# TensorE sums the three tiles of exponentials of a cross-attention itself, and the output product stands two score pairs later

## The chip, the core and the metric

The kernel runs on one core of one Trainium2 chip. The time is what the device takes for one launch, in microseconds (us). Five engines work side by side on this core: TensorE (PE) multiplies matrices and writes to PSUM, VectorE (DVE) and ScalarE (ACT) read PSUM and SBUF, GpSimd (POOL) reads SBUF, and SyncE (SP) issues most of the transfers. They wait for each other by semaphores only.

## What is computed

The reference is two layers on 16 items (B) of 112 rows (SQ) and 256 columns (D), with a context of 375 rows (SK) for each item:

```python
x = x + L0_xattn(layernorm(x), ctx)      # attention without softmax
x = x + L0_ffn(layernorm(x))             # 8 experts that choose their tokens
x = x + L1_xattn(layernorm(x), ctx)      # the part that the change touches
x = x + L1_ffn(layernorm(x))
# L1_xattn, H = 16 heads of width 16
scores = einsum('bhqd,bhkd->bhqk', Q, K) / sqrt(16)
weights = softmax(scores, axis=-1)
attn = einsum('bhqk,bhkd->bhqd', weights, V)
return attn @ Wo.T + bo
```

The change concerns the softmax's sums over the context rows and the product with `Wo`.

## The kernel before

The four parts of the two layers follow each other as stages. Within the stage of the second attention, everything goes step by step over the 16 items; n counts the steps. All engines' programs are written out by hand, in the order in which they run, and an engine runs its own list strictly in that order, waiting where a semaphore has not reached its count. Names such as `exp1_done` are semaphores.

Each item needs two kinds of scores. First come the maxima over the context: TensorE makes scores with the 112 queries on the partitions, two heads at a time (`score(n, j)`, a *score pair*, j = 0 to 7, L1559), and VectorE reduces each pair to its maxima (`two_max`, L1448). Pairs use PSUM banks 0 and 1 for even j, 2 and 3 for odd j; a pair waits until the maxima of the pair two before it are taken (`max_done`). When all eight are there, TensorE turns the maxima (`shift_turn`, the *turn*, L1566), ScalarE and VectorE form a shift (L1341, L1456), and ScalarE spreads it into extra rows of the queries `qpk` (`spread_shift`, L1344). This happens for item n+1 while item n is in the second kind of work.

Second come the weights: TensorE makes the scores again, transposed, with the context rows on the partitions (`transposed_scores`, L1582). One *unit* is four heads of one tile of 125 context rows; 12 units u = 0 to 11 make an item: for each half m of the heads, three tiles t with two groups g. ScalarE takes the exponential of each unit into `probs` (L1363). Units use three PSUM banks in turn, so unit u waits for exponential u-3. TensorE multiplies `probs` by the values, 24 matmuls for each half m (`weigh(n, m)`, L1595), into bank 7. Each such matmul uses 32 columns of the array, and four of them, g = 0 to 3, stand side by side. An f32 matmul leaves two records in the profile, so `weigh` has 48 a half.

The sums over the context are made in two parts. GpSimd adds the three tiles of a half elementwise: `half_sum` from tiles 0 and 1 (L1287), `tile_sum` from that and tile 2 (L1293), both in `add_tiles`. TensorE then folds `tile_sum` over the partitions with a table `halves` as weights (`add_up(n, m)`, a *fold*, L1608), 8 matmuls a half, into `sums` in bank 7. `add_up(n, 0)` stands at the end of step n, `add_up(n, 1)` after unit 1 of step n+1.

The rest of item n happens in step n+1. VectorE takes the reciprocal of `sums` (`invert_sums`, L1471) ahead of maximum 2, multiplies (`normalise`, `au`, L1478) ahead of maximum 3; ScalarE adds a bias after exponential 5 (`add_bias`, `aT1`, L1353); TensorE makes the product with `Wo` (`out_product`, the *out product*, L1618) into columns 384 to 511 of banks 0 and 1; and VectorE adds it to `x_all` (`add_x`, L1464).

The order is set by the numbers at the top of the program. `SCORES_AFTER` says after which unit which score pair of item n+1 stands: pair 2 after unit 2, 3 after 4, 4 after 6, 5 after 8, 6 after 10. `OUT_AT = 4` puts the out product just ahead of pair 4, and `ADD_AT = 5` puts `add_x` ahead of maximum 5. Pair 1 opens a step, pair 7 and pair 0 of item n+2 stand after `weigh(n, 0)`, then the turn, `weigh(n, 1)` and `add_up(n, 0)`.

SyncE loads the keys and queries of item n+3 once the units of step n are done; three slots of `kpk` and `qpk` are used in turn (`AHEAD`).

Of the kernel before, what the change touches and what calls it, by code (L numbers as in the profile page):

```python
# [17 lines left out]
ALU = mybir.AluOpType  # L18
# [37 lines left out]
SCORES_AFTER, OUT_AT = {2: 2, 4: 3, 6: 4, 8: 5, 10: 6}, 4  # L56
INVERT_AT, NORM_AT, ADD_AT = 2, 3, 5
# [42 lines left out]
def two_layer_kernel(nc, d, out):  # L100
# [1048 lines left out]
    tile_sum = sb(ctx, "tile_sum", [KT, KC, HC * SQ])  # L1149
    half_sum = sb(ctx, "half_sum", [KT, KC, HC * SQ])  # L1150
# [37 lines left out]
    tile_sum_done = sem(ctx, "tile_sum_done", 2 * KC)  # L1188
    pv_ps = sem(ctx, "pv_ps", KC)
    sums_ps = sem(ctx, "sums_ps")  # L1190
# [69 lines left out]
    def _(pool):  # L1260
# [21 lines left out]
        def add_tiles(n):  # L1282

            each = UNITS // KC
            for m in range(KC):
                pool.wait_ge(exp1_done.sem, exp1_done.at(n, each * m + 4))
                pool.tensor_tensor(half_sum[:, m], probs[:, m, 0], probs[:, m, 1], ALU.add)\  # L1287
                    .then_inc(tile_sum_done.sem, 1)
                pool.wait_ge(tile_sum_done.sem, tile_sum_done.at(n, 2 * m + 1))
                pool.wait_ge(exp1_done.sem, exp1_done.at(n, each * (m + 1)))  # L1290
                if n:
                    pool.wait_ge(sums_ps.sem, sums_ps.at(n - 1))
                pool.tensor_tensor(tile_sum[:, m], half_sum[:, m], probs[:, m, 2], ALU.add)\  # L1293
                    .then_inc(tile_sum_done.sem, 1)

        pool.wait_ge(qp3_done.sem, qp3_done.at(PAIRS - 1))
        for n in range(B):
            add_tiles(n)
            ahead(n)

    @block.scalar
    def _(act):
# [53 lines left out]
        def step(n):  # L1356
            for u in range(UNITS):
                m, t, g = unit(u)
                act.wait_ge(st_ps.sem, st_ps.at(n, u + 1))
                if t == 0 and g == 0 and n:  # L1360
                    act.wait_ge(pv_ps.sem, pv_ps.at(n - 1, m + 1))
                    act.wait_ge(tile_sum_done.sem, tile_sum_done.at(n - 1, 2 * (m + 1)))
# [12 lines left out]
        act.wait_ge(set_up.sem, set_up.at(0))  # L1375
        zero_padded(0)
# [132 lines left out]
    def _(pe):  # L1509
# [91 lines left out]
        def add_up(n, m):  # L1601

            pe.wait_ge(tile_sum_done.sem, tile_sum_done.at(n, 2 * (m + 1)))
            if m == 0 and n:
                pe.wait_ge(rsum_done.sem, rsum_done.at(n - 1))
            for h in range(2):
                for g in range(4):
                    ins = pe.matmul(sums[32 * g:32 * g + 32, m], halves[:, h],  # L1608
                                    tile_sum[:, m, (2 * g + h) * SQ:(2 * g + h + 1) * SQ],
                                    start=(h == 0), stop=(h == 1), tile_position=(0, 32 * g))  # L1610
            if m == KC - 1:
                ins.then_inc(sums_ps.sem, 1)
# [9 lines left out]
        def step(n):  # L1622
# [3 lines left out]
            for u in range(UNITS):  # L1626
                transposed_scores(n, u)
                if u == 1 and n:
                    add_up(n - 1, 1)
# [476 lines left out]
```

## Time and profile before

| | |
|---|---|
| median of 3 runs | 869.42 us (863.68 to 872.46) |
| profiled execution, whole | 868.87 us |
| profiled execution, span of the profile | 867.1 us |
| mean granted TensorE clock | 0.96 |
| busy in the span: TensorE | 760.4 us (88%) |
| VectorE | 477.2 us (55%) |
| GpSimd | 306.4 us (35%) |
| ScalarE | 299.4 us (35%) |

The span is the stretch from the first to the last recorded instruction; the whole execution is 1.8 us longer. All starts in this document count from the start of the span. The stage of the second attention lies between about 443 and 681 us. "PE" are matmuls, "PEld" the weight loads that overlap them. A row of the timeline merges neighbours of one kind: its "us" is from the first one's start to the last one's end, and the end of a matmul is modelled, so the time from one row's start to the next one's is what an entry takes in TensorE's queue. The releaser named behind an idle time is the one that ended last by the profile; it can be wrong where several are waited for.

### The profile page before, as it was taken

To read this page: it belongs to the slowest core of one execution; us is meant where nothing else is said; L and a number is where in the kernel's file an instruction comes from. 1 tells how busy PE (TensorE), PEld (TensorE's weight loads), DVE (VectorE), ACT (ScalarE), POOL (GpSimd) and SP (SyncE) were. 2 spreads that over 40 slices of the span, in tenths; PEclk is the share of its full clock that TensorE was granted. 3 is DMA by queue.
4 is the path that set the end of the run, shared out by engine and by line. 5 is a ranking of instruction groups with operands and counts; after the bars stand their busy time and mean duration, and the time that the engine had idled before them with its cause. 6 is when DMAs were issued, how large, how long until landed. Compare 5 with 4: busy or idle time off the path is not lost. (4 is left out here: it accounts for less than half of the span.)

```text
span 867.1 us, 16326 instructions
## 1 busy us (share of the span) xinstructions
PE 760.4 (88%) x6177; PEld 619.4 (71%) x6177; DVE 477.2 (55%) x1262; ACT 299.4 (35%) x628; POOL 306.4 (35%) x229
## 2 busy tenths in 40 slices
PE   3999999949998999996687878878788599999997
PEld 1566666624587988985666767667676489999997
DVE  1577667668860422304756677776665444555552
ACT  0111111117822311222347666665667022222221
POOL 1233332227830332316325766666666100000000
PEclk9999999969999989999898999999999699999999
DMA  9893000124785643533624776575670000000000
GB/s 284 305 170 44 22 22 22 43 68 145 205 163 107 211 140 123 164 73 86 126 48 79 127 125 124 94 134 90 121 201 2 1 1 12 12 12 11 11 11 22
DMA packets 64468, 81.46 MB, mean 94 GB/s; under 512 B 31890, under 2 KB 54802, under 8 KB 62834
## 3 DMA queue, kind: packets, MB, share of 16 engines
q1 hardware_dynamic: 61042, 70.84, 35.5%
q0 software_dynamic: 2816, 3.67, 2.4%
q10 hardware_dynamic: 544, 6.03, 2.0%
q8 instruction: 46, 0.75, 0.4%
q14 instruction: 20, 0.16, 0.1%
HBM read 60.45 MB, written 19.31 MB: 92 GB/s over the span
## 5 line engine op out<-in xcount | busy, mean ns | idle before, releaser
L1448 DVE TENSOR_REDUCE mx<-psum 112x2 f32<-112x750 f32 x128 | 116.1, 927 | 64.8 <-PE psum L1559 64.8
L1363 ACT ACTIVATE probs<-psum 125x448 f32<-125x448 f32 x192 | 91.6, 545 | 24.7 <-PE psum L1582 24.3
L507 PE MATMUL psum<-wkv,ctx_all 128*125 128x512 f32 x192 | 88.0, 609 | 13.2 <-DMA wkv<-in_wkv 13.2
L1287 POOL TENSOR_TENSOR half_sum<-probs 125x896 f32<-125x896 f32 x32 | 66.5, 2079 | 83.7 <-ACT probs L1363 83.7
L507 PEld LDWEIGHTS psum<-wkv,ctx_all 128*125 128x125 f32 x192 | 36.1, 193 | 54.2 <-issue 37.9
L1582 PEld LDWEIGHTS psum<-qpk,kpk 128*125 128x125 bf16 x768 | 64.2, 142 | 14.1 <-issue 4.4
L1769 ACT ACTIVATE relu<-psum,cols 128x224 f32<-128x224 f32 x64 | 28.7, 448 | 122.5 <-PE psum L1966 122.5
L1582 PE MATMUL psum<-qpk,kpk 128*125 128x112 bf16 x768 | 67.6, 227 | 3.2 <-ACT probs L1363 1.5
L1293 POOL TENSOR_TENSOR tile_sum<-half_sum,probs 125x896 f32<-125x896 f32 x32 | 66.9, 2090 | 2.5
L1559 PE MATMUL psum<-kpk,qpk 96*112 96x375 bf16 x256 | 63.2, 338 | 5.0 <-issue 2.4
L1098 PE MATMUL psum<-we,hT 128*112 128x256 f32 x256 | 61.2, 401 | 0.0
L1962 PE MATMUL psum<-hnT,wi 128*128 128x224 f32 x256 | 59.0, 353 | 1.1 <-DVE bias_row L1918 1.1
L1982 PE MATMUL psum<-wo,hs 128*112 128x256 f32 x256 | 58.2, 380 | 0.0
L1747 POOL TENSOR_TENSOR rs<-ve,mhalf 112x2 f32<-112x2 f32 x8 | 5.6, 698 | 145.1 <-DVE ve L1798 145.1
L1098 PEld LDWEIGHTS psum<-we,hT 128*112 128x112 f32 x256 | 47.7, 189 | 11.1
L945 ACT ACTIVATE hT<-psum,b 128x224 f32<-128x224 f32 x64 | 25.2, 444 | 79.7 <-PE psum L1083 79.7
L978 POOL DMA_INDIRECT sum_d<-outs,idx_add x16 | 29.8, 1865 | 63.5 <-DVE outs L1034 37.3
L1083 PE MATMUL psum<-rT,we 128*128 128x224 f32 x256 | 51.4, 360 | 0.9 <-ACT rT L936 0.9
L753 PE MATMUL psum<-ctx_all,wk 128*128 128x375 f32 x128 | 46.5, 508 | 6.3 <-PEq L237 4.9
L1982 PEld LDWEIGHTS psum<-wo,hs 128*112 128x112 f32 x256 | 44.8, 177 | 8.8
L1083 PEld LDWEIGHTS psum<-rT,we 128*128 128x128 f32 x256 | 49.7, 195 | 1.8 <-issue 1.1
L1962 PEld LDWEIGHTS psum<-hnT,wi 128*128 128x128 f32 x256 | 48.4, 190 | 1.7 <-DVE bias_row L1918 1.3
(203 smaller groups left out, 1411.4 us busy)
## 6 DMA issues: line engine op xcount, KB each, us to landing
we<-in_we SPq DMA_DIRECT2D x6, 2048.0 KB, 8.6
kparts_d<-kp SPq DMA_DIRECT2D x16, 562.5 KB, 5.0
kpk<-kparts_d SPq DMA_DIRECT2D x16, 562.5 KB, 6.5
ctx_all<-in_ctxT SPq DMA_DIRECT2D x16, 375.0 KB, 4.4
kpk<-kparts_d SPq DMA_DIRECT2D x16, 375.0 KB, 7.8
we<-in_we ACTq DMA_DIRECT2D x2, 2048.0 KB, 14.0
kpk<-kparts_d SPq DMA_DIRECT2D x16, 187.5 KB, 8.7
qparts_d<-qp SPq DMA_DIRECT2D x16, 168.0 KB, 3.1
```

Source lines behind the costliest of these rows:

```text
L507: ins = pe.matmul(banks[B_KV[t]][0:KT, :], ctx_of(2 * i + s)[:, k, t * KT:(t + 1) * KT], wkv0[:, k], start=(k == 0), stop=(k == KC - 1))
L753: ins = pe.matmul(banks[B_K[2 * s + m]][:, 0:SK], wk1[:, k, m * 128:(m + 1) * 128], ctx_of(n)[:, k], start=(k == 0), stop=(k == KC - 1))
L1083: ins = pe.matmul(banks[B_F[g]][:, (f % 2) * CAP:(f % 2 + 1) * CAP], we1[:, s, k, f * 128:(f + 1) * 128], rT[:, s, k], start=(k == 0), sto ...
L1098: ins = pe.matmul(banks[B_OUT[s]][0:SQ, h * D:(h + 1) * D], hT[:, s, f, h * SQ:(h + 1) * SQ], we2[:, s, f], start=(f == 0), stop=(f == FC ...
L1287: pool.tensor_tensor(half_sum[:, m], probs[:, m, 0], probs[:, m, 1], ALU.add)\
L1293: pool.tensor_tensor(tile_sum[:, m], half_sum[:, m], probs[:, m, 2], ALU.add)\
L1363: act.activation(probs[:, m, t, g * HU * SQ:(g + 1) * HU * SQ], banks[B_ST[u % 3]][0:KT, 0:HU * SQ], ACT.Exp, scale=SCALE)\
L1448: dve.tensor_reduce(mx[:, n % 2, H + 2 * j:H + 2 * j + 2], psum[0:SQ, first:first + 2, 0:SK], AX.X, ALU.max)\
L1559: ins = pe.matmul(banks[B_S[j % 2] + h][0:SQ, 0:SK], qpk[0:ROWS, s, 2 * j + h], kpk[0:ROWS, s, 2 * j + h], start=True, stop=True)
L1582: ins = pe.matmul(banks[B_ST[u % 3]][0:KT, c * SQ:(c + 1) * SQ], kpk[:, s, h, t * KT:(t + 1) * KT], qpk[:, s, h], start=True, stop=True)
L1962: pe.matmul(banks[f % 4][:, 0:2 * SQ], wi[:, k, f * 128:(f + 1) * 128], hnT[:, par, k], start=(k == 0), stop=False)
L1982: ins = pe.matmul(banks[B_Y][0:SQ, s * D:(s + 1) * D], hs[:, f, s * SQ:(s + 1) * SQ], wo[:, f], start=(f == 0), stop=(f == FC - 1))
```

## The change

GpSimd no longer adds tiles: `add_tiles`, `tile_sum`, `half_sum` and their semaphore are gone, and GpSimd has only the small add of `ahead` in each step. `add_up` now folds all three tiles of `probs` directly, 24 matmuls in place of 8 for each half, in the same nesting as `weigh`. `add_up(n, 0)` stands right behind `weigh(n, 0)`, and `add_up(n, 1)` right behind `weigh(n, 1)`, at the end of step n. `sums_ps` now counts each half, and ScalarE's wait before it overwrites a half of `probs` is on this count in place of `tile_sum_done`. `OUT_AT` goes from 4 to 6, so the out product stands behind unit 10 and ahead of pair 6; `ADD_AT` goes from 5 to 7. The wait for `x3_done`, which stood ahead of pair 6, stands ahead of pair 0 of item n+2. `probs` now lies where `tile_sum` and `half_sum` lay, over memory that the query stage used, so ScalarE waits for that stage's last subtraction on GpSimd (`qp3_done`) before its first copy into `vz`.

```diff
--- before.py
+++ after.py
@@ -53,8 +53,8 @@
 
 
 
-SCORES_AFTER, OUT_AT = {2: 2, 4: 3, 6: 4, 8: 5, 10: 6}, 4
-INVERT_AT, NORM_AT, ADD_AT = 2, 3, 5
+SCORES_AFTER, OUT_AT = {2: 2, 4: 3, 6: 4, 8: 5, 10: 6}, 6
+INVERT_AT, NORM_AT, ADD_AT = 2, 3, 7
 
 
 class Sem:
@@ -1146,8 +1146,6 @@
     earlier = sb(root, "earlier", [SQ, E1, E1])
     weights = [(la, "lora_a"), (wg1, "wg1"), (wi, "wi"), (lb, "lora_b"), (wo, "wo"), (earlier, "c_earlier")]
     ctx = ExitStack()
-    tile_sum = sb(ctx, "tile_sum", [KT, KC, HC * SQ])
-    half_sum = sb(ctx, "half_sum", [KT, KC, HC * SQ])
     probs = sb(ctx, "probs", [KT, KC, NKT, HC * SQ])
     mx = sb(ctx, "mx", [SQ, 2, 3 * H])
     high = sb(ctx, "high", [128, SQ], BF16)
@@ -1185,9 +1183,8 @@
     vz_done = sem(ctx, "vz_done")
     st_ps = sem(ctx, "st_ps", UNITS)
     exp1_done = sem(ctx, "exp1_done", UNITS)
-    tile_sum_done = sem(ctx, "tile_sum_done", 2 * KC)
     pv_ps = sem(ctx, "pv_ps", KC)
-    sums_ps = sem(ctx, "sums_ps")
+    sums_ps = sem(ctx, "sums_ps", KC)
     rsum_done = sem(ctx, "rsum_done")
     au_done = sem(ctx, "au_done")
     aT1_done = sem(ctx, "aT1_done")
@@ -1279,23 +1276,8 @@
                 pool.wait_ge(x3_done.sem, x3_done.at(b - 2))
             pool.tensor_tensor(xb1[:, b % 2], x_all[:, b], rows1[0:SQ, 0:D], ALU.add).then_inc(xb1_done.sem, 1)
 
-        def add_tiles(n):
-
-            each = UNITS // KC
-            for m in range(KC):
-                pool.wait_ge(exp1_done.sem, exp1_done.at(n, each * m + 4))
-                pool.tensor_tensor(half_sum[:, m], probs[:, m, 0], probs[:, m, 1], ALU.add)\
-                    .then_inc(tile_sum_done.sem, 1)
-                pool.wait_ge(tile_sum_done.sem, tile_sum_done.at(n, 2 * m + 1))
-                pool.wait_ge(exp1_done.sem, exp1_done.at(n, each * (m + 1)))
-                if n:
-                    pool.wait_ge(sums_ps.sem, sums_ps.at(n - 1))
-                pool.tensor_tensor(tile_sum[:, m], half_sum[:, m], probs[:, m, 2], ALU.add)\
-                    .then_inc(tile_sum_done.sem, 1)
-
         pool.wait_ge(qp3_done.sem, qp3_done.at(PAIRS - 1))
         for n in range(B):
-            add_tiles(n)
             ahead(n)
 
     @block.scalar
@@ -1359,7 +1341,7 @@
                 act.wait_ge(st_ps.sem, st_ps.at(n, u + 1))
                 if t == 0 and g == 0 and n:
                     act.wait_ge(pv_ps.sem, pv_ps.at(n - 1, m + 1))
-                    act.wait_ge(tile_sum_done.sem, tile_sum_done.at(n - 1, 2 * (m + 1)))
+                    act.wait_ge(sums_ps.sem, sums_ps.at(n - 1, m + 1))
                 act.activation(probs[:, m, t, g * HU * SQ:(g + 1) * HU * SQ],
                                banks[B_ST[u % 3]][0:KT, 0:HU * SQ], ACT.Exp, scale=SCALE)\
                     .then_inc(exp1_done.sem, 1)
@@ -1373,6 +1355,7 @@
         for b in range(V_MID + 1, B):
             keep_value(act, b, B_V)
         act.wait_ge(set_up.sem, set_up.at(0))
+        act.wait_ge(qp3_done.sem, qp3_done.at(PAIRS - 1))
         zero_padded(0)
         spread_shift(0)
         for n in range(B):
@@ -1600,16 +1583,15 @@
 
         def add_up(n, m):
 
-            pe.wait_ge(tile_sum_done.sem, tile_sum_done.at(n, 2 * (m + 1)))
             if m == 0 and n:
                 pe.wait_ge(rsum_done.sem, rsum_done.at(n - 1))
-            for h in range(2):
+            for e in range(2 * NKT):
+                h, t = divmod(e, NKT)
                 for g in range(4):
                     ins = pe.matmul(sums[32 * g:32 * g + 32, m], halves[:, h],
-                                    tile_sum[:, m, (2 * g + h) * SQ:(2 * g + h + 1) * SQ],
-                                    start=(h == 0), stop=(h == 1), tile_position=(0, 32 * g))
-            if m == KC - 1:
-                ins.then_inc(sums_ps.sem, 1)
+                                    probs[:, m, t, (2 * g + h) * SQ:(2 * g + h + 1) * SQ],
+                                    start=(e == 0), stop=(e == 2 * NKT - 1), tile_position=(0, 32 * g))
+            ins.then_inc(sums_ps.sem, 1)
 
         def out_product(n):
             pe.wait_ge(aT1_done.sem, aT1_done.at(n))
@@ -1625,26 +1607,25 @@
                 score(n + 1, 1)
             for u in range(UNITS):
                 transposed_scores(n, u)
-                if u == 1 and n:
-                    add_up(n - 1, 1)
                 j = SCORES_AFTER.get(u)
                 if j == OUT_AT and n:
                     if more:
                         pe.wait_ge(max_done.sem, max_done.at(n + 1, OUT_AT - 1))
                     out_product(n - 1)
                 if j and more:
-                    if j == OUT_AT + 2 and n:
-                        pe.wait_ge(x3_done.sem, x3_done.at(n - 1))
                     score(n + 1, j)
             weigh(n, 0)
+            add_up(n, 0)
             if more:
                 score(n + 1, H // 2 - 1)
             if n + 2 < B:
+                if n:
+                    pe.wait_ge(x3_done.sem, x3_done.at(n - 1))
                 score(n + 2, 0)
             if more:
                 shift_turn(n + 1)
             weigh(n, 1)
-            add_up(n, 0)
+            add_up(n, 1)
 
         pe.wait_ge(tables2_in.sem, tables2_in.at(AHEAD - 1))
         pe.wait_ge(qr_done.sem, qr_done.at(PAIRS - 1))
@@ -1658,7 +1639,6 @@
         pe.wait_ge(v_done.sem, v_done.at(B - 1))
         for n in range(B):
             step(n)
-        add_up(B - 1, 1)
         out_product(B - 1)
     ctx.close()
     stage.close()
```

TensorE's order at the start of a step, before. The line numbers are those of each kernel; L1559 is a score pair, L1582 transposed scores (four matmuls are a unit), L1608 a fold, L1618 the out product.

```order
L1559 MATMUL psum<-kpk,qpk 112x375 x2
L1582 MATMUL psum<-qpk,kpk 125x112 x8
L1608 MATMUL psum<-tile_sum,halves 32x112 x8
L1582 MATMUL psum<-qpk,kpk 125x112 x4
L1559 MATMUL psum<-kpk,qpk 112x375 x2
L1582 MATMUL psum<-qpk,kpk 125x112 x8
L1559 MATMUL psum<-kpk,qpk 112x375 x2
L1582 MATMUL psum<-qpk,kpk 125x112 x8
L1618 MATMUL psum<-wo,aT 112x128 x4
L1559 MATMUL psum<-kpk,qpk 112x375 x2
L1582 MATMUL psum<-qpk,kpk 125x112 x8
L1559 MATMUL psum<-kpk,qpk 112x375 x2
```

The same place after. Here L1542 is a score pair, L1565 transposed scores, L1600 the out product; the list runs to pair 6.

```order
L1542 MATMUL psum<-kpk,qpk 112x375 x2
L1565 MATMUL psum<-qpk,kpk 125x112 x12
L1542 MATMUL psum<-kpk,qpk 112x375 x2
L1565 MATMUL psum<-qpk,kpk 125x112 x8
L1542 MATMUL psum<-kpk,qpk 112x375 x2
L1565 MATMUL psum<-qpk,kpk 125x112 x8
L1542 MATMUL psum<-kpk,qpk 112x375 x2
L1565 MATMUL psum<-qpk,kpk 125x112 x8
L1542 MATMUL psum<-kpk,qpk 112x375 x2
L1565 MATMUL psum<-qpk,kpk 125x112 x8
L1600 MATMUL psum<-wo,aT 112x128 x4
L1542 MATMUL psum<-kpk,qpk 112x375 x2
```

The fold between units 1 and 2 is gone, so three units stand in one piece, and the out product has moved from behind unit 6 to behind unit 10.

TensorE's order at the end of a step and the start of the next, before: `weigh` (L1595), pairs 7 and 0 together, the turn (L1566), `weigh`, a fold of 8, and pair 1 of the next step with units 0 and 1 and the fold of half 1.

```order
L1595 MATMUL psum<-probs,vz 32x112 x24
L1559 MATMUL psum<-kpk,qpk 112x375 x4
L1566 MATMUL psum<-ident,mx 32x112 x2
L1595 MATMUL psum<-probs,vz 32x112 x24
L1608 MATMUL psum<-tile_sum,halves 32x112 x8
L1559 MATMUL psum<-kpk,qpk 112x375 x2
L1582 MATMUL psum<-qpk,kpk 125x112 x8
L1608 MATMUL psum<-tile_sum,halves 32x112 x8
```

The same place after, with L1578 `weigh`, L1591 the fold, L1549 the turn.

```order
L1578 MATMUL psum<-probs,vz 32x112 x24
L1591 MATMUL psum<-probs,halves 32x112 x24
L1542 MATMUL psum<-kpk,qpk 112x375 x4
L1549 MATMUL psum<-ident,mx 32x112 x2
L1578 MATMUL psum<-probs,vz 32x112 x24
L1591 MATMUL psum<-probs,halves 32x112 x24
L1542 MATMUL psum<-kpk,qpk 112x375 x2
```

A fold of 24 now stands between `weigh` and pair 7, and another one ends the step.

## Rows read from the trace of the kernel before

**Rows 1.** Stretches (length, busy us and count by engine, granted clock, DMA); waits in 460:682.
```profile
512.43:525.97 13.54, 11.13 (x206) 9.46 (x205) 9.61 (x12) 9.06 (x20) 9.31 (x7) 1.00 0.62 115
...
583.00:590.00 7.00, 5.37 (x43) 4.92 (x41) 4.28 (x7) 3.68 (x10) 4.15 (x2) 0.76 0.31 45
...
PE psum L1618 <- DVE mx L1448: 22.7, 14, 1.6
```

**Rows 2.** Timeline, TensorE, one step (start, us, engine, line, what, count [idle before]).
```profile
512.43 0.53 PE L1559 MATMUL psum<-kpk,qpk 96*112 96x375 bf16 x2
512.79 0.62 PE L1582 MATMUL psum<-qpk,kpk 128*125 128x112 bf16 x8
513.34 0.59 PE L1608 MATMUL psum<-tile_sum,halves 125*32 125x112 f32 x16
...
514.13 0.49 PE L1559 MATMUL psum<-kpk,qpk 96*112 96x375 bf16 x2
514.46 0.62 PE L1582 MATMUL psum<-qpk,kpk 128*125 128x112 bf16 x8
514.91 0.49 PE L1559 MATMUL psum<-kpk,qpk 96*112 96x375 bf16 x2
...
517.62 1.10 PE L1618 MATMUL psum<-wo,aT 128*112 128x128 f32 x8 [1.64 <-DVE mx L1448]
518.55 0.49 PE L1559 MATMUL psum<-kpk,qpk 96*112 96x375 bf16 x2
...
520.40 0.53 PE L1559 MATMUL psum<-kpk,qpk 96*112 96x375 bf16 x2
520.77 0.39 PE L1582 MATMUL psum<-qpk,kpk 128*125 128x112 bf16 x4
521.08 1.36 PE L1595 MATMUL psum<-probs,vz 125*32 125x112 f32 x48
522.37 0.85 PE L1559 MATMUL psum<-kpk,qpk 96*112 96x375 bf16 x4
523.93 0.28 PE L1566 MATMUL psum<-ident,mx 112*32 112x112 f32 x1 [0.71 <-DVE mx L1448]
...
525.97 0.53 PE L1559 MATMUL psum<-kpk,qpk 96*112 96x375 bf16 x2
```

**Rows 3.** Timeline, VectorE, the same step.
```profile
512.99 0.94 DVE L1448 TENSOR_REDUCE mx<-psum 112x2 f32<-112x750 f32 x1 [1.36 <-PE psum L1559]
514.00 1.56 DVE L1471 RECIPROCAL rsum<-psum 128x224 f32<-128x224 f32 x1
515.47 0.88 DVE L1448 TENSOR_REDUCE mx<-psum 112x2 f32<-112x750 f32 x1
516.38 0.39 DVE L1478 TENSOR_TENSOR au<-psum,rsum 128x224 f32<-128x224 f32 x1
516.69 0.93 DVE L1448 TENSOR_REDUCE mx<-psum 112x2 f32<-112x750 f32 x1
...
520.26 1.77 DVE L1448 TENSOR_REDUCE mx<-psum 112x2 f32<-112x750 f32 x2
```

**Rows 4.** Timeline, ScalarE, the same step.
```profile
513.47 2.83 ACT L1363 ACTIVATE probs<-psum 125x448 f32<-125x448 f32 x6
516.80 0.67 ACT L1353 ACTIVATE aT<-au,cols 128x112 f32<-128x112 f32 x2 [0.51 <-DVE au L1478]
```

**Rows 5.** Timeline, GpSimd's last subtraction and ScalarE's first copy into `vz`.
```profile
443.70 1.03 POOL L1273 TENSOR_TENSOR qp<-qr,qp 128x448 bf16<-128x448 f32 x1 [1.09 <-ACT qp L1322]
...
453.43 0.93 ACT L1333 ACTIVATE vz<-ctx_all 125x384 f32<-125x384 f32 x2
```

**Rows 6.** Timeline, the last step.
```profile
670.33 2.51 PE L1595 MATMUL psum<-probs,vz 125*32 125x112 f32 x96
...
674.75 0.59 PE L1608 MATMUL psum<-tile_sum,halves 125*32 125x112 f32 x16 [1.52 <-POOL tile_sum L1293]
675.40 1.56 DVE L1471 RECIPROCAL rsum<-psum 128x224 f32<-128x224 f32 x1 [6.26 <-PE psum L1608]
```

## The prediction

> **What bounds the kernel now.** I read the page first, then the stretches table, then the timeline of one step engine by engine. The stretches table takes one step of the attention stage, 512.43 to 525.97, which is 13.54 us long: TensorE is busy 11.13 of it, VectorE 9.61, ScalarE 9.06, GpSimd 9.31, and the granted clock is 1.00, the 2.4 GHz level [rows 1]. No engine is full, so the length is set by a loop through several engines. Call T0 the start of the score pair 1 that opens a step (512.43). TensorE's timeline gives the marks: out product at T0+5.19, score pair 4 at 6.12, pair 6 at 7.97, the last unit of transposed scores at 8.34, `weigh` of half 0 at 8.65, pair 7 and the next pair 0 at 9.94, the shift turn at 11.50, the next T0 at 13.54 [rows 2]. Two of them follow a wait: 1.64 us before the out product, 0.71 before the turn. The profile names a maximum as releaser of the first. VectorE's and ScalarE's timelines show what ended last: pair 1, maximum (0.56), reciprocal (1.57), maximum, product `au` (3.95), then ScalarE's bias `aT`, 4.37 to 5.04, and the out product at 5.19 [rows 3, 4]. The reciprocal waits for GpSimd's sum as TensorE folds it after unit 1: those 16 records end at 513.34 + 0.59 = 513.93, and it starts at 514.00 [rows 2, 3]. The turn's wait is pair 7 going through its maximum: 1.56 us from pair 7 to the turn, of which the two score pairs cover about half. So the loop is: VectorE's chain up to the out product, then TensorE's queue up to pair 7, then pair 7's maximum, then TensorE's queue to the next T0.
>
> **GpSimd's adds go.** Four adds a step leave, two into `half_sum` and two into `tile_sum`, nearly all of GpSimd's 9.31 us [rows 1]. GpSimd is not in the loop except through the fold, so nothing is gained beyond what follows. Its last subtraction of the query parts starts at 443.70 and takes 1.03; ScalarE's new wait for it stands before the copy into `vz`, which starts at 453.43 in any case [rows 5]. Price nothing; if that cover were gone, GpSimd would still have to be 8.7 us later to be felt.
>
> **TensorE sums three tiles.** A fold was 8 matmuls, 16 records; it is now 24 matmuls, 48 records, of the form of `weigh` (125 rows, 32 columns of weights, 112 moving, f32). 48 records of `weigh` take 1.36 us and 96 take 2.51 [rows 2, 6], so 48 more cost 1.15, or 0.024 a record. A fold was 0.38 and is 1.15. The low end is 48 x (2.51 - 0.26) / 95 = 1.14, `weigh`'s own pace without the 0.26 in which the last record drains; below that it cannot go, as it is the same count of the same records. High end: if the pace were that of the lone fold of 16, 0.59 [rows 2], 48 would take 1.77. I take 1.15, since the new fold follows `weigh` directly with the same forms. The trace has no row in which the moving operand of a fold is the exponentials themselves, but `weigh` reads exactly these.
>
> **One steady step after.** The three places where TensorE's order changes are the fold after unit 1 (gone), the out product (from after unit 6 to after unit 10) and a fold of half 0 between `weigh` and pair 7, with the fold of half 1 in place of half 0's at the end.
>
> First the chain on VectorE. Pair 1 at 0, maximum at 0.56. The sums were finished before T0, so the reciprocal follows at the spacing of neighbours, 0.88 (two in 1.77): 1.44. Then the spacings before: 1.47 to maximum 2 (2.91), 0.91 to `au` (3.82), 0.31 to maximum 3 (4.13), 0.88 to maximum 4 (5.01) [rows 3]. So this chain gains 0.13.
>
> Now TensorE. Units 0 to 2 run from 0.36, pair 2, units 3 and 4, pair 3, units 5 and 6 follow. Unit u needs exponential u-3; the exponentials can start at 0.8, once unit 0 is out, and go at 0.47 (six in 2.83) [rows 4], so exponential 3 is done at 0.8 + 3 x 0.47 + 0.55 = 2.76 and unit 6 is through near 3.1. Pair 4 needs maximum 2, done at 2.91 + 0.94 = 3.85: it starts at 3.9, where TensorE was ready near 3.1. Pair 5 needs maximum 3, done at 5.07: 5.13, where TensorE was ready near 4.7. This is what is late next: a wait of some 0.8 and one of 0.4 in front of the scores. They were there before too, inside the 1.64. A score pair takes 0.33 and two units 0.45 [rows 2]: unit 10 would be out at 5.91; it needs exponential 7. `aT` starts when `au` is done (4.25), takes 0.67, and two exponentials after it end near 5.9, so unit 10 leaves TensorE near 6.1. The out product needs maximum 4 (5.95) and `aT` (4.92): neither holds it. It starts at 6.1.
>
> From there TensorE's queue runs: out product 0.93 (517.62 to 518.55), pair 6 0.37, unit 11 0.31, `weigh` 1.29 (521.08 to 522.37), the new fold 1.15 [rows 2]. Sum 6.1 + 4.05 = 10.15 for pair 7, against 9.94: 0.21 later. What is queued behind the fold is pair 7, and for that wait maximum 7, the turn, ScalarE's spread and the next step: the fold is wholly on the path. The new wait for `x_all` before the next pair 0 is met, since that add is done by about 9. Pair 7 to the turn stays 1.56: 11.71. The turn, `weigh` and a fold of 16 records took 2.04; now 48 records: 2.04 + 0.77 = 2.81. Next T0 at 14.52, against 13.54: **0.98 us longer per step**. The spread and its exponentials no longer hold unit 0, so nothing shortens the far end. Key loads, triggered by unit 11, go out earlier in the step, so their queue gets more room, not less.
>
> **The sum.** Steps 1 to 14 are of this kind: 14 x 0.98 = 13.7. Step 0 has no out product to wait for, so it pays both folds whole: 1.15 + 0.77 = 1.9. Step 15 has no scores. There `weigh` started at 670.33 and the reciprocal at 675.40 after a 1.52 wait for GpSimd [rows 6]; now 192 records run from about the same point: 670.33 + 191 x 0.024 + 0.26 + 0.06 = 675.2, a gain of 0.2. So 1.9 + 13.7 - 0.2 = 15.4.
>
> The clock: in 583 to 590 it was 0.76 [rows 1], after the usual 1.64 us of idling ahead of an out product, so TensorE fell to 1.2 GHz for part of it. At most 7.0 x 0.24 = 1.7 us went there. The new step has no single wait over 0.9 and 1.5 us more work, so I take half back, 0.8.
> The Trainium skill (TensorE: Matmul & The Clock Gate, Part 1) says that the slow level is the default and that activity releases it. By that rule the whole 1.7 would come back and the sum be 13.7; the trace agrees only in part, since 14 steps idle up to 1.6 there [rows 1] and the clock is 1.00 in the step that stands above.
>
> 15.4 - 0.8 = 14.6. The profiled execution took 868.87 (span 867.1), so 883.5; on the median of 869.42 it is 884.0. I predict 884.
>
> **Rivals.** (1) Not slower: the stall goes and nothing takes its place. If TensorE's own queue were the only bound in the first half of the step, that is, if pairs 4 and 5 did not meet late maxima, the step would be 13.54 - 1.64 - 0.76 + 2.30 = 13.44, so -1.4 over 14 steps; with 1.9, -0.2 and -0.8 that is 0.5 less: 868.4 from the profiled execution, 869 on the median. It decides if pair 5 can start before T0+4.2. For it: the named wait is the largest of the step, and VectorE is busy only 9.61 of 13.54. Against it: reciprocal, `au` and three reductions in a row fill VectorE from 0.56 to 5.07 with no gap. (2) Faster: the wait before the turn (0.71) goes as well: 12.73 a step, -11.3, with 1.9, -0.2 and -0.8 a total of 10.4 less: 859 on the median. Against: pair 7 still stands directly ahead of the turn, with less than its 1.56 in between. (3) Much slower: folds at the pace of the lone one, 1.77: 0.62 twice a step over 15 steps, 18.6 more, 902. Against: 96 records in a row keep 0.024. A half-way case would be 893. That the change does not do what it says can't be: the order of instructions shows it.
>
> **How the numbers follow.** The forecast has a chance of 0.74, rival 1 0.14, rival 2 0.05, rival 3 0.07. The forecast's own range, from 0.2 a step less or more and the clock either way, is 879 to 888. To hold 8 in 10 the range goes down into rival 1 and up a little into rival 3: 869 to 890. About 1%, 8.7 us, is what a measurement of this kernel can tell from no change, its three runs being 863.68 to 872.46. Faster by over 1%: 0.06. Within 1%: 0.17. Slower: 0.77 (the forecast, rival 3 and a few cases between).
>
> **What would show it.** Right: step period near 14.5; 48-record folds of 1.36 or so; no wait named at the out product; idle time of 0.8 and 0.4 us before pairs 4 and 5 with a maximum as releaser; pair 7 near T0+10.15; the wait before the turn still near 0.7; reductions 0.94 as before with GpSimd idle. Wrong: a period below 13.8, pair 4 or 5 not waiting, or folds of over 1.6 us.

## The result and the profile after

The changed kernel takes 901.9 us (median of 4 runs, 900.94 to 908.55) against 870.46 (863.68 to 872.46): the ratio is 1.0398, with an interval from 1.0331 to 1.0466. That is slower, as forecast, but by 31 us and not by the 14.6 that I had added, and outside the range. The span of the profiled execution went from 867.1 to 899.1 us.

The page of the changed kernel first: GpSimd has almost nothing left to do in the stage, the granted clock dips more often, and more blocks of instructions were loaded.

```profile
span 899.1 us, 18261 instructions
...
POOL 1233232248613233252400000000000000000000
...
PEclk9999999879989999997998999989999799999999
...
q8 instruction: 54, 0.88, 0.5%
```

The same queue on the page of the kernel before moved 46 packets, of 16 KB each:

```profile
q8 instruction: 46, 0.75, 0.4%
```

A step that nothing disturbs, on TensorE's timeline (start, us, engine, line, what, count, idle before and its releaser), against [rows 2]. L1542 is a score pair, L1565 transposed scores, L1600 the output product, L1578 `weigh`, L1591 the fold, L1549 the turn:

```profile
538.74 0.53 PE L1542 MATMUL psum<-kpk,qpk 96*112 96x375 bf16 x2
539.11 0.85 PE L1565 MATMUL psum<-qpk,kpk 128*125 128x112 bf16 x12
...
542.56 0.53 PE L1542 MATMUL psum<-kpk,qpk 96*112 96x375 bf16 x2 [0.62 <-DVE mx L1431]
...
543.83 0.53 PE L1542 MATMUL psum<-kpk,qpk 96*112 96x375 bf16 x2 [0.28 <-DVE mx L1431]
...
544.81 1.08 PE L1600 MATMUL psum<-wo,aT 128*112 128x128 f32 x8
545.74 0.49 PE L1542 MATMUL psum<-kpk,qpk 96*112 96x375 bf16 x2
546.06 0.39 PE L1565 MATMUL psum<-qpk,kpk 128*125 128x112 bf16 x4
546.38 1.36 PE L1578 MATMUL psum<-probs,vz 125*32 125x112 f32 x48
547.55 1.33 PE L1591 MATMUL psum<-probs,halves 125*32 125x112 f32 x48
548.82 0.85 PE L1542 MATMUL psum<-kpk,qpk 96*112 96x375 bf16 x4
550.37 0.28 PE L1549 MATMUL psum<-ident,mx 112*32 112x112 f32 x1 [0.71 <-DVE mx L1431]
...
553.18 0.53 PE L1542 MATMUL psum<-kpk,qpk 96*112 96x375 bf16 x2
```

T0 is 538.74, the next one 553.18: 14.44 us, where I had worked out 14.52 and [rows 2] has 13.54. Pair 4 starts at T0+3.82 behind a wait of 0.62, pair 5 at 5.09 behind one of 0.28, the output product at 6.07 with no wait. The new fold takes 1.27 to pair 7's start, pair 7 comes at 10.08 and the turn at 11.63, still behind a wait of 0.71.

VectorE in the same step, against [rows 3]:

```profile
539.31 0.94 DVE L1431 TENSOR_REDUCE mx<-psum 112x2 f32<-112x750 f32 x1 [2.13 <-PE psum L1542]
540.16 1.55 DVE L1454 RECIPROCAL rsum<-psum 128x224 f32<-128x224 f32 x1
541.63 0.88 DVE L1431 TENSOR_REDUCE mx<-psum 112x2 f32<-112x750 f32 x1
542.54 0.39 DVE L1461 TENSOR_TENSOR au<-psum,rsum 128x224 f32<-128x224 f32 x1
542.84 2.62 DVE L1431 TENSOR_REDUCE mx<-psum 112x2 f32<-112x750 f32 x3
```

Maximum 1 at 0.57, reciprocal at 1.42, `au` at 3.80, then three maxima in one run: the chain that I had drawn, with reductions as long as before although GpSimd stands idle.

So the steady step is as predicted. The rest is in steps that are not steady. Of the 13 intervals between the reciprocals of consecutive full steps, five last 14.43 or 14.44 us. The others last 14.77, 15.14, 15.39, 16.32, 16.36, 17.90, 20.21 and 21.68: 22.3 us more than 13 undisturbed steps, where the kernel before lost 2.1 so. TensorE's timeline shows the cause in ten rows like these, with "issue" behind the idle time, that is, TensorE waited for nothing that the profile knows:

```profile
475.26 0.25 PE L1565 MATMUL psum<-qpk,kpk 128*125 128x112 bf16 x1 [2.94 <-issue]
...
488.22 1.20 PE L1591 MATMUL psum<-probs,halves 125*32 125x112 f32 x39
492.57 0.35 PE L1591 MATMUL psum<-probs,halves 125*32 125x112 f32 x2 [3.15 <-issue]
...
603.94 0.84 PE L1565 MATMUL psum<-qpk,kpk 128*125 128x112 bf16 x7 [3.56 <-issue]
...
636.33 0.58 PE L1591 MATMUL psum<-probs,halves 125*32 125x112 f32 x13 [3.43 <-issue]
```

The second wait stands in the middle of a fold, 2 matmul records ahead of its end; others are in the middle of transposed scores. No semaphore is waited for there. The ten waits add up to 20.1 us; the kernel before has two of 0.5. The table of stretches, with the borders at the ends of consecutive waits, shows what they have in common (length, then busy us and count for TensorE's matmuls and its weight loads, and so on):

```profile
475.20:492.50 17.30, 13.44 (x253) 11.87 (x253) 7.54 (x10) 8.31 (x17) 0.73 (x1) 0.83 0.57 94
492.50:507.30 14.80, 12.69 (x253) 10.54 (x252) 9.52 (x12) 8.61 (x19) 0.73 (x1) 1.00 0.55 101
507.30:523.30 16.00, 12.63 (x252) 10.58 (x253) 9.52 (x12) 9.10 (x20) 0.73 (x1) 1.00 0.71 123
523.30:573.60 50.30, 44.23 (x885) 37.27 (x884) 33.94 (x43) 31.06 (x68) 2.21 (x3) 1.00 0.56 98
```

From one wait to the next there are 253 + 253 or 252 + 253 records. The fourth stretch, over which no long wait falls, has 885 + 884 = 1769, which is 7 x 252.7. The waits sit on a grid of some 253 recorded TensorE instructions. These counts leave out TensorE's bare waits on semaphores, which the trace does keep: 7 in the undisturbed step, beside its 536 matmuls and weight loads. Counted with them, neighbouring waits are 512 instructions apart and those at the ends of the fourth stretch 1793, give or take one: twice and seven times 256.

The trace also has the packets of the queue named instruction. Two stretches of the changed kernel, 486 to 488 and 488 to 490, lie within a load of keys and queries (queue, kind: packets, MB, share of the 16 DMA engines' time):

```profile
q1 hardware_dynamic: 66, 0.30, 101.7%
...
q1 hardware_dynamic: 81, 0.39, 94.2%
q8 instruction: 1, 0.02, 4.2%
```

TensorE enters a block at 484.41 and has worked it off at 489.42. Only at 489.62 does the next instruction packet start. It takes 1.35 us, and TensorE goes on at 492.57, 1.60 us after the packet's end. The other nine waits end in the same way, 1.40 to 1.56 us after the end of an instruction packet. In all ten kernels of this document that have such waits in the steps of this stage, 47 waits of over 0.25 us, it is 1.22 to 1.73 us, and every one of the 47 stands at the same place of a block: 137 or 138 instructions past a multiple of 256, counted from the first recorded TensorE instruction. Below I take that place as the border at which TensorE enters a block.

### The profile page after: what moved, and what is told of

It reads as the page before. It is cut to its first block and busy times, and to the rows that moved or that the text cites. A ratio compares the mean times of both kernels' runs of the same rounds, so it can differ in the third digit from the quotient of the medians.

```text
span 899.1 us, 18261 instructions
## 1 busy us (share of the span) xinstructions
PE 790.0 (88%) x7201; PEld 646.7 (72%) x7201; DVE 476.8 (53%) x1262; ACT 297.7 (33%) x628; POOL 173.9 (19%) x165
## 5 line engine op out<-in xcount | busy, mean ns | idle before, releaser
L1345 ACT ACTIVATE probs<-psum 125x448 f32<-125x448 f32 x192 | 89.8, 550 | 32.5 <-PE psum L1565 32.4
L1565 PE MATMUL psum<-qpk,kpk 128*125 128x112 bf16 x768 | 73.8, 237 | 13.4 <-issue 10.6
L1565 PEld LDWEIGHTS psum<-qpk,kpk 128*125 128x125 bf16 x768 | 67.3, 151 | 25.1 <-issue 8.6
L1542 PE MATMUL psum<-kpk,qpk 96*112 96x375 bf16 x256 | 66.5, 353 | 13.3 <-DVE mx L1431 10.1
L1277 POOL TENSOR_TENSOR xb<-x_all,rows 112x256 f32<-112x256 f32 x16 | 11.7, 732 | 236.1 <-DVE x_all L1447 236.0
L1591 PE MATMUL psum<-probs,halves 125*32 125x112 f32 x1536 | 47.8, 259 | 9.6 <-issue 9.6
L1591 PEld LDWEIGHTS psum<-probs,halves 125*32 125x32 f32 x1536 | 41.7, 110 | 10.6 <-issue 10.6
L1853 DVE SCALAR_TENSOR_TENSOR hs<-psum,neg_bi,relu 128x224 f32<-128x224 f32 x64 | 28.8, 450 | 37.7 <-PE psum L1952 36.1
```

Source lines behind the costliest of these rows:

```text
L1345: act.activation(probs[:, m, t, g * HU * SQ:(g + 1) * HU * SQ], banks[B_ST[u % 3]][0:KT, 0:HU * SQ], ACT.Exp, scale=SCALE)\
L1542: ins = pe.matmul(banks[B_S[j % 2] + h][0:SQ, 0:SK], qpk[0:ROWS, s, 2 * j + h], kpk[0:ROWS, s, 2 * j + h], start=True, stop=True)
L1565: ins = pe.matmul(banks[B_ST[u % 3]][0:KT, c * SQ:(c + 1) * SQ], kpk[:, s, h, t * KT:(t + 1) * KT], qpk[:, s, h], start=True, stop=True)
L1591: ins = pe.matmul(sums[32 * g:32 * g + 32, m], halves[:, h], probs[:, m, t, (2 * g + h) * SQ:(2 * g + h + 1) * SQ], start=(e == 0), stop=( ...
L1853: dve.scalar_tensor_tensor(hs[:, f], banks[f % 4][:, 0:2 * SQ], neg_bi[:, f:f + 1], relu1[:, f % 4], ALU.max, ALU.add).then_inc(hs_done.se ...
```

## The experiments

Three theories stood. Theory A: at the border of a block TensorE waits for its own instructions, because the block is fetched while the key and query loads hold the DMA engines. Theory B: the new list uses up blocks faster than they can be fetched at all. Theory C: it is the data, the folds that read the exponentials directly. "Small loads" below leave part of the keys and queries out. The kernel before was timed beside each set: 868.86, 867.97 and 868.91 us.

**e1: the changed kernel, small loads.**

```diff
+        part = slice(0, 64) if b >= AHEAD else slice(0, H // KC * SK)
-            sp.dma_start(kpk[...], rows_of(kparts_d[b], r))
+            sp.dma_start(kpk[...][:, :, part], rows_of(kparts_d[b], r)[:, :, part])
```

> The changed kernel with the key and query loads of items 3 to 15 cut to 64 columns of each half (the other columns keep the data of an earlier item; number of loads and semaphores as before). Seen in the changed kernel: waits of 0.3 to 3.6 us that the profile puts down to issue, 506 recorded TensorE instructions or a multiple apart, 20.1 us in all. Theory A (TensorE waits for its own instructions, and the block it needs is fetched behind the key and query loads): these waits go, all steps are near 14.4 us, total 880 us (878 to 885). Theory B (the dense runs of folds and value products use up instructions faster than they can be fetched at all): the waits stay, total 898 to 902 us. Theory C (the waits come from the exponentials read by the folds, not from fetching): 898 to 902 us.

Measured: 876.19 us (872.97 to 877.67), 1.0085 of the kernel before (1.0059 to 1.011). No issue wait over 0.2 us is left in the stage, and all 13 intervals are 14.43 or 14.44 us. VectorE's timeline, the reciprocals of two neighbouring steps:

```profile
511.75 1.55 DVE L1456 RECIPROCAL rsum<-psum 128x224 f32<-128x224 f32 x1
...
526.18 1.55 DVE L1456 RECIPROCAL rsum<-psum 128x224 f32<-128x224 f32 x1
```

Theories B and C fall: the instructions, their order and the folds' operands are those of the changed kernel. Between the first and the last reciprocal the two traces differ by 235.41 - 211.86 = 23.5 us, more than the 20.1 of named waits; the granted clock is part of that, 0.98 from 473 to 700 against 0.96. Another 4.2 us lie ahead of the first reciprocal, and those are not the loads' doing: VectorE's memset that opens the stage already starts 4.9 us earlier (436.36 against 441.21), well ahead of the first load that is cut here, which SyncE issues at 464.47 in the changed kernel. The instruction packets hardly differ in length, 0.88 to 1.44 us against 0.88 to 2.01 between 473 and 682, but in their start: 2 of 31 start over 2 us after TensorE has entered a block, where in the changed kernel it is 17 of 28, the latest 7.15 us after.

**e2: the changed kernel, folds over one tile only** (the sums leave out tiles 1 and 2).

```diff
-            for e in range(2 * NKT):
-                h, t = divmod(e, NKT)
+            for h in range(2):
+                t = 0
```

> The changed kernel, but each fold sums only tile 0 (8 matmuls in place of 24), so tiles 1 and 2 are left out of the sums. Everything else is where the change put it. Each step loses 128 TensorE records of matmuls and weight loads. Theories A and B (fetching): the issue waits go nearly all, steps last 14.43 - 2 x 0.77 = 12.9 us, total 858 to 864 us. Theory C (folds that read the exponentials): folds of 8 still read them, waits of some 10 us or more stay, total 868 to 875 us.

Measured: 858.27 us (857.66 to 858.86), ratio 0.9868 (0.9836 to 0.9899). The steps last 12.90 us, as worked out. One long wait is left, and it stands in a fold:

```profile
487.05 0.35 PE L1591 MATMUL psum<-probs,halves 125*32 125x112 f32 x2 [2.83 <-issue]
```

With 128 records fewer a step the loads are the same, yet nine of ten waits are gone. The packets are still late: 13 of 24 start over 2 us after TensorE has entered a block, the latest 6.31. So they are in the kernel before, 14 of 24 and up to 6.46, and it has only two waits of 0.5. Late packets alone are not enough; the block in hand must also be worked off quickly. With small loads the shortest blocks of the full steps last 4.7 us in the changed kernel (e1) and 5.5 in the kernel before (e10).

**e3: the kernel before with only the output product moved.**

```diff
-SCORES_AFTER, OUT_AT = {2: 2, 4: 3, 6: 4, 8: 5, 10: 6}, 4
-INVERT_AT, NORM_AT, ADD_AT = 2, 3, 5
+SCORES_AFTER, OUT_AT = {2: 2, 4: 3, 6: 4, 8: 5, 10: 6}, 6
+INVERT_AT, NORM_AT, ADD_AT = 2, 3, 7
```

> The kernel before with only the output product moved behind unit 10 (and its add behind maximum 6, and the wait for it ahead of the next pair 0). GpSimd still adds the tiles. By the marks of my prediction: pair 4 near T0+4.0, pair 5 near 5.3, out product near 6.25, pair 7 near 9.15 in place of 9.94, turn 10.7, so steps of 12.75 us in place of 13.54: total 859 us (856 to 862). Rival: VectorE's chain is what sets the step whatever the order, then 868 to 872 us. Under theory A the number of TensorE instructions is that of before, so no new issue waits, though denser steps may bring a few (up to 4 us).

Measured: 860.93 us (858.28 to 863.02), ratio 0.9896 (0.9856 to 0.9936). An undisturbed step takes 12.68 us (expected 12.75). TensorE's timeline, first one of the two long waits, then marks of a step that begins at 538.55:

```profile
503.30 0.56 PE L1559 MATMUL psum<-kpk,qpk 96*112 96x375 bf16 x1 [1.69 <-issue]
...
542.53 0.53 PE L1559 MATMUL psum<-kpk,qpk 96*112 96x375 bf16 x2 [0.42 <-DVE mx L1448]
...
544.79 1.09 PE L1618 MATMUL psum<-wo,aT 128*112 128x128 f32 x8
...
547.64 0.85 PE L1559 MATMUL psum<-kpk,qpk 96*112 96x375 bf16 x4
549.20 0.28 PE L1566 MATMUL psum<-ident,mx 112*32 112x112 f32 x1 [0.71 <-DVE mx L1448]
```

Pair 4 at T0+3.98, the output product at 6.24, pair 7 at 9.09, turn at 10.65. Two intervals of 17.20 and 17.26 us, each with one issue wait (1.69 and 1.94) and slow TensorE rows around it, keep back some of the gain. The half of the change that moves the product was a gain by itself, some 1%.

**e4: the changed kernel, loads issued at the end of the step.**

```diff
                 sp.wait_ge(st_ps.sem, st_ps.at(n))
+                sp.wait_ge(sums_ps.sem, sums_ps.at(n))
                 load_keys(sp, n + AHEAD)
```

> The changed kernel with the key and query loads of item n+3 issued when the folds of step n are done (end of the step) in place of when unit 11 is out, nothing left out. Theory A: the dense part of TensorE's list no longer meets the loads, so the issue waits mostly go or move to the start of the step: total 880 to 892 us. If pair 0 then waits for late keys, that is named as a DMA wait ahead of a score pair. Theories B and C: 898 to 903 us.

Measured: 884.71 us (883.96 to 885.95), ratio 1.0178 (1.0144 to 1.0211). Nothing is left out here, and 17 us come back by when the loads start. The issue waits shrink from 20.1 to 3.8 us; in their place pair 0 waits for queries, 4.2 us in eight waits. One of each on TensorE's timeline:

```profile
569.93 0.50 PE L1543 MATMUL psum<-kpk,qpk 96*112 96x375 bf16 x2 [0.70 <-DMA qpk<-qparts_d]
...
585.41 0.39 PE L1592 MATMUL psum<-probs,halves 125*32 125x112 f32 x5 [1.53 <-issue]
```

**e5: the changed kernel with the fold of half 0 in the wait before the turn.**

```diff
             weigh(n, 0)
-            add_up(n, 0)
...
                 score(n + 2, 0)
+            add_up(n, 0)
             if more:
                 shift_turn(n + 1)
```

> The changed kernel with the fold of half 0 standing between pair 0 and the turn, where TensorE waits for maximum 7 in any case, in place of ahead of pair 7. If the fold of half 0 is on the path only because pair 7 is queued behind it, steps shrink by about 0.85 us (0.71 of named wait plus the pause at the change of semaphore) to 13.6, and the total by 12 us: 890 us (885 to 895), with the fetch waits of theory A still there. Rival: the wait only moves to another place and the total stays 899 to 903 us.

Measured: 910.68 us (907.76 to 913.72), ratio 1.0499 (1.045 to 1.0548): the expected total was missed by 20 us and on the wrong side of the changed kernel. Yet three intervals of 13.67 or 13.68 in a row show the step that I had worked out (13.6). What grew are the issue waits, the longest to 5.4 us (columns: us in total, times, longest):

```profile
PE psum L1591 <- issue: 19.8, 5, 5.4
PE psum L1565 <- issue: 16.2, 5, 5.4
```

Those two lines are 36.0 us against 20.1 in the changed kernel. A shorter step with the same instructions asks for blocks sooner (in e11, the same order with small loads, the shortest block of the full steps lasts 3.1 us), and the loads are in the way as long as before.

**e6: the changed kernel with the product back ahead of pair 4.**

```diff
-SCORES_AFTER, OUT_AT = {2: 2, 4: 3, 6: 4, 8: 5, 10: 6}, 6
+SCORES_AFTER, OUT_AT = {2: 2, 4: 3, 6: 4, 8: 5, 10: 6}, 4
```

(with the add and its wait as before). 

> The changed kernel with the output product back where it was (ahead of pair 4, its add ahead of maximum 5, the wait for it ahead of pair 6). By my marks the product then starts near T0+5.0 behind aT, pair 4 near 5.95 and pair 7 0.45 us later than in the changed kernel: steps of 14.9 us, total 907 us (904 to 911), the fetch waits as they were. Rival: the place of the product does nothing, 900 to 903 us.

Measured: 927.01 us (925.66 to 933.27), ratio 1.0694 (1.0656 to 1.0733), 20 us over what I expected. The wait ahead of the product is back with 1.83 us, and behind it the score pair is slow:

```profile
557.17 1.34 PE L1600 MATMUL psum<-wo,aT 128*112 128x128 f32 x8 [1.83 <-DVE mx L1431]
558.30 0.83 PE L1542 MATMUL psum<-kpk,qpk 96*112 96x375 bf16 x2
...
590.30 1.10 PE L1600 MATMUL psum<-wo,aT 128*112 128x128 f32 x8 [1.83 <-DVE mx L1431]
```

In such a step a score pair's row is 0.83 us long in place of 0.49, and the granted clock from 555 to 572 is 0.90, so TensorE is at 1.2 GHz for a part of it. It falls in one step after another: five of the intervals are 16.56 to 16.81 us, where the two shortest of the full steps are 15.3. The wait alone does not decide it: it is 1.83 at 590.30 too, in one of the steps of 15.3, and there the granted clock from 587 to 602 is 1.00. My 14.9 had no clock in it and was 0.4 short besides.

**e7: the kernel before, product late (e3) and the fold of half 0 in the wait before the turn.** The diff is those of e3 and e5 together.

> The kernel before (GpSimd adds the tiles) with the late output product of e3 and, besides, the fold of half 0 between pair 0 and the turn. GpSimd's sum of half 0 is ready near T0+7.4, so the fold of 0.38 us fits wholly into the wait: steps of 12.3 us in place of 12.68, total 855.5 us (852 to 859). If denser steps bring more fetch waits (theory A), up to 861.

Measured: 858.44 us (853.85 to 866.51), ratio 0.9886 (0.9846 to 0.9925). The step is 12.60 us, only 0.08 less than in e3. TensorE's timeline shows where the expected 0.38 went:

```profile
544.92 0.59 PE L1608 MATMUL psum<-tile_sum,halves 125*32 125x112 f32 x16
545.70 0.28 PE L1566 MATMUL psum<-ident,mx 112*32 112x112 f32 x1 [0.19 <-DVE mx L1448]
...
547.35 0.53 PE L1559 MATMUL psum<-kpk,qpk 96*112 96x375 bf16 x2
547.97 0.67 PE L1582 MATMUL psum<-qpk,kpk 128*125 128x112 bf16 x8
```

The fold is in the wait as meant, but unit 0 now starts 0.62 after pair 1 in place of 0.36: TensorE has arrived before ScalarE's spread of the shift, and that became the bound. The list of waits names it for the weight loads of the transposed scores, 15 times, where in e3 it is once 0.4 us:

```profile
PEld psum L1582 <- ACT qpk L1344: 6.9, 15, 0.8
```

**e8: e7 with the loads after the turn.**

```diff
                 sp.wait_ge(st_ps.sem, st_ps.at(n))
+                sp.wait_ge(turn_ps.sem, turn_ps.at(n + 1))
                 load_keys(sp, n + AHEAD)
```

> As e7, with the key and query loads of item n+3 issued after the turn of item n+1 (some 3 us later in the step). Theory A: the loads meet another part of TensorE's list; in e4 a shift to the end of the step took most of the fetch waits away at the price of late queries. Here I expect the fetch waits at or below those of e7 and no late queries: total 850 to 857 us. If the rest of the fetch waits is not a matter of where the loads stand, it equals e7 within 2 us.

Measured: 854.1 us (852.82 to 855.35), ratio 0.985 (0.9814 to 0.9886): the lowest median of all, and faster than both kernels. Its undisturbed step is e7's 12.60. What is left of waits in the stage, from the list of waits:

```profile
PE psum L1560 <- DMA qpk<-qparts_d: 1.7, 4, 0.6
...
PE psum L1596 <- issue: 0.3, 1, 0.3
```

Its median is 4 us below e7's, and its runs spread over 2.5 us where e7's spread over 12.7. Whether that is the loads' place cannot be settled by these medians, as e7's fastest run is 853.85.

**e9: the changed kernel with 32 more matmuls once, ahead of the first turn.**

```diff
+            for r in range(32 if n == 0 else 0):
+                pe.matmul(turned, mx[:, n % 2, 0:2 * H], ident[0:SQ, 0:SQ], start=True, stop=True,
+                          tile_position=(0, ROWS))
```

> The changed kernel with 32 more matmuls of 32 x 112, f32 (128 TensorE records) once, ahead of the first turn; their result is overwritten. Theory A says that the issue waits stand at the borders of blocks of TensorE's own instructions: they must then be 506 recorded instructions or a multiple apart as before, but each stands 128 records earlier in the program, at another matmul of the step than in the changed kernel (whose second one stood 2 matmul records ahead of the end of a fold). If they belong to places of the step or to the data, they stay at the same matmuls. Total: 3 to 7 us for the added matmuls, and more or less waiting as the borders fall: 895 to 915 us.

Measured: 905.56 us (899.94 to 907.51), ratio 1.0395 (1.031 to 1.0479). The table of stretches from wait to wait, and one of the waits on TensorE's timeline:

```profile
529.00:544.20 15.20, 10.87 (x253) 9.65 (x253) 7.58 (x9) 7.10 (x14) 0.73 (x1) 1.00 0.56 101
544.20:559.60 15.40, 12.27 (x253) 11.01 (x253) 7.45 (x10) 7.71 (x16) 0.73 (x1) 0.89 0.55 95
...
592.20:674.20 82.00, 68.00 (x1390) 58.20 (x1390) 51.37 (x64) 46.57 (x99) 3.65 (x5) 0.98 0.61 113
...
544.30 0.32 PE L1542 MATMUL psum<-kpk,qpk 96*112 96x375 bf16 x1 [3.64 <-issue]
```

The waits keep their distance, 506 records, or 2780 in the last stretch, which is 11 x 252.7. But they stand at other matmuls: this one is between the two matmuls of pair 2, and one more stands ahead of pair 1, where the changed kernel has none. They belong to the count of instructions, not to a place in the step. Counted with the waits on semaphores, all six stand at 137 or 138 past a multiple of 256 like those of the changed kernel, and so 128 instructions earlier in the program, as theory A had it.

**e10: the kernel before, small loads.** The diff is that of e1.

> The kernel before with the same cut loads as in e1. What the fetching and the loads cost there: its two issue waits of 0.5 us and the start of the stage, some 4 us earlier in e1's trace than in the changed kernel's. Steps of 13.54 us throughout: total 862 to 866 us. The difference to e1 (876.2) is then the price of the change with no fetch waits: my 15.4 us less the clock, so 11 to 15 us.

Measured: 867.88 us (866.29 to 872.91), ratio 0.9988 (0.9958 to 1.0018): no change, where I had expected 3 to 7 us less. Its issue waits go, and 12 of its 13 intervals are 13.54 to 13.55, and the total does not move: the earlier first reciprocal in e1's trace, 468.44, from which I had expected a gain here too, was not the loads' doing (this one comes at 472.13, that of the kernel before at 472.99). The difference to e1 is 876.19 - 867.88 = 8.3 us.

**e11: e5, small loads.** The diffs of e5 and e1.

> e5 with the cut loads of e1. In e5 the undisturbed steps were 13.67 us but the issue waits grew to 36 us. Theory A: with the loads cut all steps are near 13.67, total 876.2 - 14 x 0.77 = 865 us (863 to 869). Otherwise the waits come from the denser list itself and 10 us or more of them stay.

Measured: 866.94 us (862.84 to 869.02), ratio 0.9975 (0.9945 to 1.0005). All 13 intervals are 13.67 or 13.68. So e5's 36 us of waits hung on the loads too, and without them e5's order would cost nothing against the kernel before. That is not to say that the folds are free: the step is 13.67 against 13.54, and the later product, which saved 0.86 us a step in e3, is in it.

## Why the prediction was wrong

**VectorE's chain, the waits before pairs 4 and 5, the product that waits for nothing: right.** Worked out 3.9, 5.13 and 6.1 after T0; measured 3.82, 5.09 and 6.07. The named waits are 0.62 and 0.28, somewhat less than my 0.8 and 0.4.

**The price of a fold: right.** I had 1.15 and the high end 1.77. From the new fold's first record to the next pair it is 548.82 - 547.55 = 1.27 with the pause before the pair, and the row is 1.33 long. That puts rival 3 aside, though its 902 is the time that was measured: it named folds at a slow pace, and no fold is slow.

**The steady step: right.** 14.52 against 14.44, so 0.90 more per step in place of 0.98. e1 less e10, 8.3 us, is what the change costs where no fetch wait is in it. The 13 steady steps make 13 x 0.89 = 11.6 us between the reciprocals, less 1.3 for one interval of 14.81 in e10's trace; the rest of the distance lies outside them. VectorE's small memset that opens the stage starts at 442.99 in the kernel before, at 441.21 in the changed one, at 440.14 in e10 and at 436.36 in e1, so the stages ahead, which nobody touched, differ by some us from one execution to the next, and comparisons of a few us between these kernels carry that. The 1.9 for step 0 can't be seen apart from it: from that memset to the first reciprocal it is 31.38 us in the changed kernel and 30.00 in the kernel before, 1.4 more, though the granted clock in that stretch is 0.95 in the changed kernel and 0.89 in the kernel before, so that the 1.9 is neither confirmed nor refuted. The gain of 0.2 in the last step: its interval is 11.08 in e1 and 11.47 in e10, but 12.35 in the changed kernel, where the granted clock in it is 0.86, against 10.87 in the kernel before.

**The clock: wrong in sign.** I took 0.8 us back because the new step has shorter waits. The fetch waits of up to 3.6 us are longer than any that I had counted, and from 473 to 494 the granted clock is 0.84. Where no fetch wait comes (e1) all 13 intervals are undisturbed, and the slower step of the kernel before, an interval of 14.80 around 583 to 590, is not there: so far as this one trace shows, the term itself was right, and it was outweighed.

**The step that failed** is the sentence "Key loads, triggered by unit 11, go out earlier in the step, so their queue gets more room, not less", and with it that I priced the 1.5 us of new matmuls by TensorE's time alone. 128 more records a step are 128 more instructions to bring in, by packets that start late while the loads move. The kernel before had nearly enough time in each block to hide that, and the new list has not. I looked at whether the keys come in time, and not at what the keys hold up. The trace of before had both signs, two waits of 0.5 us put down to issue in the middle of the stage and a queue named instruction on the page; I used neither. The missing term is 20.1 us of named waits, with the clock behind them: 22.3 us of disturbed intervals, less the 2.1 of before. Then 11.6 for the 13 steady steps, 22.3 - 2.1 = 20.2, and 1.1 for the last two intervals make 32.9, and between first and last reciprocal the two traces differ by 235.41 - 202.41 = 33.0.

Shown by runs: the waits go when the bytes of the loads go (e1, e11), mostly go when the loads start at another time (e4), mostly go when the list is shorter (e2), grow when the same list runs in less time (e5), and move with the count of instructions (e9). The Trainium skill (Runtime: NRT & Kernel Launch, Instruction fetch mechanics) says that each engine's instructions come in blocks of 256, fetched over a DMA queue while the block before runs. This case's trace agrees: 256 instructions to a block, of which some 253 are matmuls and weight loads and the rest waits on semaphores, and packets of 16 KB, of which 27 of 28 in the changed kernel start once TensorE has entered the block ahead of theirs. The same section calls the cost mostly hidden; here single waits are 3.6 us, and 5.4 in e5. The packets' times show where the time goes: not into the transfer, 2.01 us at the most, but ahead of it, up to 7.15 us from the entry into a block to the start of the packet, where with small loads the median is 0.4. Not shown is what happens in that time, whether the request stands in a queue behind the loads or goes out late itself, since the trace has no record of it; nor what TensorE does in the 1.2 to 1.7 us after the packet's end.

Rival 1 did not come: pairs 4 and 5 do wait. But its number did in another way: e11 shows that a better place for the fold of half 0 brings the step to 13.67.

## What to carry to other kernels

Matmuls added to a dense stretch can cost more than their time: each is an instruction to be brought in as well, and where large loads run at the same moment TensorE may stand still at the border of a block. Count the instructions of a step as one counts its bytes, look in the trace for idle time that is put down to issue in the middle of a group, and if the distance between such waits is a multiple of one number of instructions (256 here, 253 without the waits on semaphores), move the loads or shorten the list before anything else. And try the halves of a double change apart: the later product was worth 1% (e3) and is part of the fastest version (e8, 854.1 us), while the sums on TensorE cost more than that gained.

## What the runs showed of the hardware that was not expected

A wait of TensorE for its instructions can be 5.4 us long (e5), with 256 instructions to a block. The packets that bring them start up to 6.46 us after the entry into a block even in the kernel before, where two waits of 0.5 us are all that shows of it. A wait of 1.83 us ahead of the product, in steps of 16.6 us, came with the 1.2 GHz level in one step after another (e6), though not in every one, while the kernel before, with 1.64 us in steps of 13.54, met it once between 473 and 664. And a faster order can be the slower kernel: e5's steps are 0.76 us shorter than the changed kernel's, and it is 9 us slower.
